# Row norm behind the MLP in rounds one and two: centring and gain moved from one VectorE pass to a ScalarE pass and a later 512-wide VectorE product

## The reference, cut to what matters

```
for _ in range(3):
    prev = slots
    q = _ln(slots, lnq_g, lnq_b) @ wq + bq
    attn = softmax(k q^T / scale) + EPS_ATTN;  attn = attn / attn.sum(axis=1)
    slots = (attn^T v) @ wu + bu + prev
    h = _ln(slots, lnm_g, lnm_b) @ w1 + b1
    slots = gelu(h) @ w2 + b2 + slots
    slots = _ln(slots + x_cls[:, None, :], lnp_g, lnp_b)
```

## Time and profile before

| | before |
|---|---|
| median of 3 runs | 337.73 us (337.51 to 338.34) |
| the profiled execution's own time | 337.5 us |
| its span | 335.7 us |
| TensorE matmul busy | 315.6 us (94%) |
| VectorE busy | 278.6 us (83%) |
| ScalarE busy | 228.0 us (68%) |
| GpSimd busy | 217.2 us (65%) |
| granted TensorE clock | 0.994 |

### The profile page before, as it was taken

The page is one execution under the profiler, slowest core; times in us unless marked ns, Lnnn a source line. Parts: engine busy times, 40 slices in busy tenths (PEclk is TensorE's granted clock), DMA queues, the critical chain, the costliest instruction groups (busy, mean ns, idle before and its releaser), DMA issues. The chain is left out here.

```text
span 335.7 us, 6155 instructions
## 1 busy us (share of the span) xinstructions
PE 315.6 (94%) x1758; PEld 259.8 (77%) x1758; DVE 278.6 (83%) x816; ACT 228.0 (68%) x502; POOL 217.2 (65%) x417
## 2 busy tenths in 40 slices
PE   8999999999999989999998999999986799999995
PEld 7888887888888868888877777787862577777774
DVE  4699968899899889999999999977779478888763
ACT  2369985967467867776588764776655497777871
POOL 3269965266689754557987646668766888566331
PEclk9999999999999999999999999999999799999999
DMA  8998000000000000000000000000000000000001
GB/s 284 326 309 365 6 1 0 2 0 1 3 0 0 3 1 0 2 1 1 2 0 0 3 0 2 2 1 0 2 0 0 1 34 33 32 31 2 34 31 62
DMA packets 5312, 13.24 MB, mean 39 GB/s; under 512 B 672, under 2 KB 672, under 8 KB 4896
## 3 DMA queue, kind: packets, MB, share of 16 engines
q1 hardware_dynamic: 4160, 10.88, 8.9%
q10 hardware_dynamic: 1120, 1.98, 1.6%
HBM read 10.76 MB, written 2.10 MB: 38 GB/s over the span
## 5 line engine op out<-in xcount | busy, mean ns | idle before, releaser
L284 DVE BATCH_NORM_STATS2 stats<-S 128x6 f32<-128x256 f32 x112 | 42.1, 417 | 9.7 <-DMA S<-ctx 3.5
L335 PE MATMUL ps_mid<-XT,KT 128*128 128x256 f32 x192 | 46.1, 383 | 3.8 <-ACT XT L351 3.8
L335 PE MATMUL ps_low<-V,PR 128*128 128x257 f32 x192 | 46.4, 384 | 1.1 <-DVE PR L867 0.9
L335 PE MATMUL ps_low<-wn,GT 128*128 128x256 f32 x192 | 45.6, 380 | 1.0 <-ACT GT L655 1.0
L335 PE MATMUL ps_mid<-XT,wt 128*128 128x256 f32 x192 | 45.6, 380 | 0.8 <-ACT XT L351 0.7
L335 PEld LDWEIGHTS ps_low<-V,PR 128*128 128x128 f32 x192 | 35.8, 190 | 8.5 <-DVE PR L867 3.7
L652 ACT ACTIVATE PR<-ps_mid,nmax 128x256 f32<-128x256 f32 x48 | 22.4, 472 | 29.2 <-DVE nmax L877 29.1
L302 POOL TENSOR_TENSOR lnm_ab<-lnm_mv,mhalf 128x2 f32<-128x2 f32 x24 | 17.4, 727 | 37.2 <-DVE lnm_mv L292 37.2
L335 PEld LDWEIGHTS ps_mid<-XT,KT 128*128 128x128 f32 x192 | 34.6, 190 | 8.9 <-ACT XT L351 5.2
L335 PEld LDWEIGHTS ps_low<-wn,GT 128*128 128x128 f32 x192 | 36.1, 190 | 6.6 <-ACT GT L655 1.8
L335 PEld LDWEIGHTS ps_mid<-XT,wt 128*128 128x128 f32 x192 | 34.7, 190 | 5.1 <-ACT XT L351 1.2
(11 more groups left out here) (126 smaller groups left out, 697.7 us busy)
## 6 DMA issues: line engine op xcount, KB each, us to landing
S<-ctx SPq DMA_DIRECT2D x8, 256.0 KB, 3.7
X<-x SPq DMA_DIRECT2D x8, 256.0 KB, 3.5
out<-X SPq DMA_DIRECT2D x8, 256.0 KB, 2.0
rowv<-rows SPq DMA_DIRECT2D x1, 1920.0 KB, 10.0
wf<-w_fc_t SPq DMA_DIRECT2D x1, 1024.0 KB, 11.9
wf<-w_proj_t SPq DMA_DIRECT2D x1, 1024.0 KB, 13.8
wt<-w_tr ACTq DMA_DIRECT2D x1, 512.0 KB, 4.3
wn<-w_nat ACTq DMA_DIRECT2D x1, 512.0 KB, 5.4
```

The costliest lines, as they stand in the source:

```text
L284: dve.bn_stats(ln.st[:, at, j, 0:6], tiles[:, j]).then_inc(ln.stats_done, 1)
L335: last = pe.matmul(dst(m), lhs_t[:, c, m * P:(m + 1) * P], rhs[:, c, 0:n], start=(c == 0), stop=(c == 1))
```

## The change

In rounds one and two VectorE no longer runs `centre_gain` at step 10 + b. GpSimd makes a shift as well as a scale for `lnp` (three instructions instead of one). ScalarE writes unit rows from `S` with scale and shift (L311, as for the other norms). VectorE then multiplies both tiles by `lnp_g` in one 512-wide tensor_tensor, in step 12 + b, ahead of the tail; the gain row is read twice through a broadcast view. GpSimd's `lnp_b` add in the same step waits for that product (`p_gained`), where it waited for ScalarE (`p_scaled`).

```diff
+        def both_rows(r):
+            return r[:, None, :].broadcast_to([P, J2, D])
...
             def norm_coefs(t, s, last):
                 for r, half, b in staged(t, s, LOW, last):
-                    ln_coef(pool, lnp if half else lnm, r * B + b, b, shift=not half)
+                    ln_coef(pool, lnp if half else lnm, r * B + b, b, shift=not (half and last))
...
                 if it := item(t, s, 3 if last else 4, last):
                     r, half, b = it
                     if half == 1:
-                        pool.wait_ge(p_scaled, r * (J2 * B) + (J2 * b + J2))
                         if last:
+                            pool.wait_ge(p_scaled, (ROUNDS - 1) * B + (J2 * b + J2))
...
                         else:
+                            pool.wait_ge(p_gained, r * B + (b + 1))
                             for j in range(J2):
                                 pool.tensor_tensor(Y[:, b, j], XH[:, b, j], row("lnp_b"), ALU.add)\
                                     .then_inc(y_ready, 1)
...
                         ln_apply(act, lnm, r * B + b, b, S[:, b], XH[:, b], xm_ready)
+                    elif r < ROUNDS - 1:
+                        ln_apply(act, lnp, r * B + b, b, S[:, b], XH[:, b], p_scaled)
                     else:
                         act.wait_ge(lnp.coef, r * B + (b + 1))
-                        act.wait_ge(p_gained, r * (J2 * B) + (J2 * b + J2))
+                        act.wait_ge(p_gained, r * B + (J2 * b + J2))
...
+                if (it := item(t, s, 4, last)) and not last:
+                    r, half, b = it
+                    if half == 1:
+                        dve.wait_ge(p_scaled, r * B + (b + 1))
+                        dve.tensor_tensor(XH[:, b], XH[:, b], both_rows(row("lnp_g")), ALU.mult).then_inc(p_gained, 1)
...
-                    if half == 1:
+                    if half == 1 and last:
                         centre_gain(dve, lnp, r * B + b, b, S[:, b], XH[:, b], row("lnp_g"), p_gained)
```

## The result

The changed kernel takes 340.53 us (median of 4, 340.21 to 340.98) against 337.78 us for the kernel before (4 runs), a ratio of 1.0061 with a 95% interval of 1.0033 to 1.0089. I had forecast 337.6 us and no change to speak of; the range ended at 340.0. The profiled execution took 340.32 us, its span is 338.5 us, 2.8 longer than before. The medians differ by 2.75 us; the ratio is that of the comparison of runs and stands for 2.1 us, and both lie within the interval. Executions of one kernel come with a mean granted clock of 0.995 or 0.989, the second some 1 to 2 us longer, so medians are read together with one place in the trace ahead of the stretch where that clock falls.

What follows compares the result with a forecast made beforehand. It took TensorE's beat of about 3.9 us a step as the bound, VectorE after step 18 of round two. Round one -0.35, round two +0.2: -0.15 us on 337.5, median 0.23 above, so 337.6 us; range 336.2 to 340.0.

Steps and rivals of the forecast that it cites:

- What bounds the kernel: Rounds one and two: TensorE's beat of about 3.9 us a step, with few stops; VectorE after step 18 of round two.
- the stop of step 15: TensorE's low product waiting for GELU, in rounds one and two: 0.85 us longer.
- Absorption behind step 17: Steps 18 to 20 absorb up to 0.7 us of lateness; step 20 wins 0.35 us in round one.
- VectorE's relief: VectorE's work falls by 3.7 us, hidden; rival that it reaches the path: 336.2 or 334.0 us, together chance 0.15.
- Step 15: GpSimd's full queue shifts by 0.52 us per added block; TensorE's release moves from 170.72 to 171.57 us.
- GpSimd now needs 1.42 + 1.21 + 1.21 = 3.84 us in a step against a beat of 3.9. It keeps up: Steps 15 to 17: Y add and two coefficient blocks just fit, leaving the middle product of step 19 0.7 us late.
- The row maxima of steps 18 and 19: Sign of error on VectorE: if later than today, the lateness was more than VectorE could absorb.
- the rival of GpSimd falling behind: GpSimd's blocks cost 0.75 us more than today, and both rounds pay: 2.3 us, 339.9 us; chance 0.27.
- one such meeting, at shift_x: Round two: shift_x on VectorE waits once for the GpSimd Y add starting beside it, 0.5 us.
- The Y add of step 18 now comes behind the product and so behind PR: Round two: PR on VectorE runs without the GpSimd add beside it, 0.75 us less.
- The product's price: The 512-wide VectorE product takes 0.68 us, about 0.60 of it occupied; floor 676 ns, ceiling 934 ns.
- The window of 200 to 220 us: Round two, VectorE busy 17.80 of 20 us: if this stretch changes its length, contention there was missed.

Runs made afterwards that it cites:

- short coefficient blocks: The changed kernel with GpSimd's lnp block one pow again and ScalarE reading the shift of lnm, the product kept: 336.31 us, ratio 0.9944.
- maximum: The changed kernel with the product replaced by a VectorE maximum over the same 512 elements, lnp gain left out: 337.61 us, ratio 0.9981.
- two halves: The changed kernel with the product as two tensor_tensor of 256 in place of one of 512: 339.0 us, ratio 1.0025.
- each half alone: GpSimd's three lnp instructions added to the kernel before: 337.58 us; the changed kernel with one pow for lnp, product kept: 336.31 us.
- GELU first: The kernel before with ScalarE running GELU right behind the copy of XT, ahead of the norm passes, in steps 10 to 16: 338.37 us, ratio 1.0018.
- the negated lnq mean: The kernel before with the negated mean of lnq made by VectorE instead of GpSimd: 338.83 us, ratio 1.0028.
- the maximum and the longer lnp block: The changed kernel with a maximum replacing the product, lnp gain left out, and two unread GpSimd instructions added in each lnp block: 339.55 us.

## Why the prediction was wrong, point by point

*What bounds the kernel, and the stop of step 15.* Right. The kernel with GpSimd's three instructions alone has the stop longer by 0.84 us, forecast 0.85. That holds for the instructions without the product: in the changed kernel the low product of step 15 was 2.06 us late.

*Absorption behind step 17.* Right as a mechanism: that kernel is level again at step 20. In the changed kernel, too, 2.45 us of lateness at step 19 become 1.4 at step 20.

*VectorE's relief.* Right: 3.9 us less work for 3.7 forecast, and mostly hidden, as said. The exactness is in part luck, for the rows hold things that weren't reckoned: w costs 1.2 us more, and PR and `below` together 1.9 less. It shows as 1.7 us where GpSimd keeps its beat (short coefficient blocks).

*The step that failed: the price of GpSimd's step, in "Step 15" and in "GpSimd now needs 1.42 + 1.21 + 1.21 = 3.84 us in a step against a beat of 3.9. It keeps up".* In steps 13 and 14 the Y add held the queue for 1.55 us, the lnq block for 1.55 (102.29 to 103.84) and the lnp block for 1.08, which is 4.18 to 4.19 us. The sum had the price of the instructions and not that of their meeting with the new product. The meetings began in step 11. The prediction's own terms put the Y adds of steps 12 to 15 late by 0, 0.52, 0.80 and 1.13 us (the last is 0.80 + 3.84, less the 3.51 from 168.88 to 172.39 us in the kernel before); measured in round one were 0.47, 1.30, 1.95 and 2.63. In steps 15 to 17, of which the sentence speaks, the queue did keep up, at 3.80 to 3.90 us a step, with 2.63 us of lateness already in it. The lateness at step 19 became 2.45 us instead of 0.7, over the 1 us or so that is absorbed, in each of two rounds. The row maxima of steps 18 and 19 came 1.03 and 0.56 us later in round one (122.23 for 121.20, 125.39 for 124.83), which the prediction had named as the sign of this.

I had put this down as the rival of GpSimd falling behind, at 0.27 and 339.9 us, with the right threshold (about 3.9 us of work a step). Its price was 0.6 too low; its chance was the error. The earlier trace rows held the evidence: w at 0.97 for 0.46, and the pow of 0.93. I charged one such meeting, at shift_x, where the product's place in each of five steps, right before a Y add and beside a pow, called for one a step. (The product meets them in 4 steps at full price; in steps 15 to 17 it falls beside the short instructions, 0.43 and 0.54 us for 0.19 and 0.20.) I had also taken the slowed pow as a bound of GpSimd's cost in calm terms, and not asked what slows it.

*A second misreading, of little weight.* "The Y add of step 18 now comes behind the product and so behind PR": the product stands at the very head of VectorE's step, ahead of rinv and PR. PR of step 18 still ran beside the Y add, 1.09 us, not 0.61. The run with the product moved to where I had placed it is not faster, so this reading didn't hide the loss.

*The product's price.* 0.65 us alone (forecast 0.68), 735 ns on average with its waits. The Trainium skill, "VectorE: DVE Perf Modes", the section on SBUF-source ops, gives 691 ns, which is an estimate for this product; the 648 ns of the kernel with short coefficients are a little less.

*The window of 200 to 220 us.* VectorE is busy for 18.33 us there, 17.80 in the earlier trace rows. The stretch has only moved by 2.8 us; the lateness is the same at its beginning and behind it.

What stays open is the share of VectorE's own waits (the product at 1.04, w at 0.97 more often: 605 ns on average for 529) in the 2.9 us between product and maximum, whether the second tensor read or the writing does it, and how much depends on where in the VectorE instruction the GpSimd instruction starts.

## What to carry to other kernels

When work moves onto an engine whose queue is nearly full in the critical steps, add up that engine's step against the beat, with the meetings included: an instruction that is cheap for one engine can lengthen another engine's queue. Before giving VectorE a product with two SBUF operands, look at what GpSimd does in that moment; here two halves, or an operation on one tensor, hurt less. And test the parts of a change apart: here each half alone was a gain or nothing, and only the two together cost 2.75 us.

## What the runs showed of the hardware

A GpSimd instruction on two numbers per partition is slowed too, and more than a wide one: pow went from 0.70 to 1.05 and 1.15 us when it started beside a 512-wide two-tensor VectorE instruction, and the pair of 256-wide adds from 1.46 to 1.59 beside w. Pow was not slowed beside a one-tensor reduction of 641 ns, nor beside the `centre_gain` that started 0.05 us ahead of it.

In the rounds, stops of TensorE of up to 1.56 us cost their length, while longer ones can cost more. Behind the stop of 3.25 us the granted clock of the windows was 0.80 and 0.77, a part of the time at the lower of the two levels (1.2 and 2.4 GHz), where behind stops of 1.3 us it stayed at 1.00. The length of the stop doesn't decide by itself: in the kernel before with GELU first, the clock in the 4 us from 120 us was 0.64 behind a stop of 1.87 us in round one, and it stayed at 1.00 behind one of 2.08 us in round two. Behind the rounds nearly all kernels have a stop of 4.0 us (262 us in the kernel before; 3.6 with the negated lnq mean), and there the granted clock differed between executions with the same stop. Windows of the changed kernel, and of the one with the maximum and the longer lnp block:

```profile
262.00:280.00 18.00, 14.68 (x99) 11.03 (x100) 11.53 (x24) 12.23 (x24) 16.30 (x27) 0.91 0.04 16
```

```profile
262.00:280.00 18.00, 14.95 (x93) 11.41 (x94) 10.55 (x21) 10.59 (x20) 13.34 (x28) 0.81 0.05 16
```

Where it was 0.81, the end came later by more than the rounds explain: that execution took 341.99 us, where the median of its kernel is 339.55. That is why the shifts above are read ahead of 262 us as well as from the medians.
